# A two-layer transformer kernel: set-up buffers in another order, denser value blocks, other orders in its first and last iterations

## The reference

```
m = silu(mod) @ w_ada + b_ada                    # 9 vectors per batch: shifts, scales, gates
h = ln(x)*(1+sc)+sh; x += self_attn(h)*g         # windows of 128 rows, shifted by 64      (stage A)
h = ln(x)*(1+sc)+sh; x += topk_cross_attn(h)*g   # 77 context rows, softmax over the 16 largest scores (stage B)
h = ln(x)*(1+sc)+sh; x += swiglu(h)*g            # 256 -> 2*1024 -> 256                     (stage C)
xq = ada_ln(x); xkv = ada_ln(context)
x = x + cross_attn(xq, xkv) @ Wp + bp            # plain softmax over 77 context rows       (stage D)
```

## Time and profile before

| | us |
|---|---|
| runs, median of 3 | 1008.47 |
| profiled execution, own time | 1009.15 |
| its span, first to last instruction | 1007.0 |
| PE busy in the span | 955.5 |
| DVE busy | 851.8 |
| ACT busy | 782.0 |
| POOL busy | 682.3 |

### The profile page before, as it was taken

One profiled execution on the slowest core, in us unless ns is written; L12 is line 12 of the kernel. 1 busy time (PEld: TensorE's weight loads), 2 busy tenths in 40 slices (PEclk: granted clock), 3 DMA queues, 4 the chain that ended last, 5 costly groups with the idle time before them and its releaser, 6 DMA issues.

```text
span 1007.0 us, 32855 instructions
## 1 busy us (share of the span) xinstructions
PE 955.5 (95%) x10750; PEld 836.9 (83%) x10750; DVE 851.8 (85%) x4268; ACT 782.0 (78%) x1679; POOL 682.3 (68%) x1092
## 2 busy tenths in 40 slices
PE   6776899999999999999999999999999999999996
PEld 3564688899988888989898888888999888887784
DVE  1467899999999999999999999999999999889643
ACT  1244678888888888888888888888888888887764
POOL 1158356877777777777777777777777777777763
PEclk9678999999999999999999999999999999999999
DMA  8255400000000000000100011000100100000000
GB/s 281 67 97 89 143 22 7 14 21 23 23 24 23 23 24 13 17 18 23 24 23 23 23 23 23 18 11 19 23 23 23 23 23 18 18 7 7 7 7 16
DMA packets 72153, 33.66 MB, mean 33 GB/s; under 512 B 56520, under 2 KB 68961, under 8 KB 71346
## 3 DMA queue, kind: packets, MB, share of 16 engines
q1 hardware_dynamic: 71986, 31.57, 12.6%
HBM read 22.64 MB, written 8.91 MB: 31 GB/s over the span
## 4 chain that ended last, share of the span: by engine, by line
PE 84%; issue 5%; DVE 4%; POOL 4%; ACT 2%; DMA 0%; DVEq 0%; SPq 0%; POOLq 0%; ACTq 0%
PE ps L2211 22%; PE ps L2222 10%; PE ps L2090 8%; PE ps L2200 8%; PE ps L2176 7%; PE ps L2189 6%; PE ps L2162 4%; PE ps L2138 3%; PE ps L2121 3%; PE ps L2151 3%; PE ps L2101 3%; PE ps L2111 2%; PE ps L2079 2%; PE ps L2011 1%; DVE mx_A L1412 1%
## 5 line engine op out<-in xcount | busy, mean ns | idle before, releaser
L2211 PE MATMUL ps<-hT_C,w_m_sb 128*128 128x128 f32 x2048 | 264.5, 278 | 1.2 <-DVE hidden_C L1555 0.8
L2211 PEld LDWEIGHTS ps<-hT_C,w_m_sb 128*128 128x128 f32 x2048 | 247.4, 192 | 13.7 <-issue 6.8
L934 ACT ACTIVATE silu_C<-ps,cols_sb 128x128 f32<-128x128 f32 x256 | 93.5, 367 | 71.8 <-PE ps L2211 67.7
L2222 PE MATMUL ps<-w_m_sb,hidden_C 128*128 128x256 f32 x512 | 121.1, 379 | 0.0
L601 POOL TENSOR_TENSOR p_B<-p_B,rc_B 128x616 f32<-128x616 f32 x64 | 77.8, 1217 | 51.3 <-DVE p_B L1473 50.7
L1465 DVE MATCH_REPLACE8 scores_left_B<-mx_B,scores_left_B 128x77 f32<-128x77 f32 x512 | 107.7, 223 | 0.0
L1461 DVE MATCH_REPLACE8 scores_left_B<-mx_B,scores_B 128x77 f32<-128x77 f32 x512 | 107.3, 224 | 0.0
L2222 PEld LDWEIGHTS ps<-w_m_sb,hidden_C 128*128 128x128 f32 x512 | 92.4, 190 | 9.9
L1412 DVE TENSOR_REDUCE mx_A<-ps 128x8 f32<-128x1024 f32 x64 | 75.5, 1221 | 22.6 <-PE ps L2121 22.6
L1555 DVE SCALAR_TENSOR_TENSOR hidden_C<-ps,cols_sb,silu_C 128x128 f32<-128x128 f32 x256 | 83.3, 337 | 10.1 <-ACT silu_C L934 9.8
L601 POOL TENSOR_TENSOR p_D<-scores_D,rc_D 128x616 f32<-128x616 f32 x63 | 76.8, 1222 | 16.2 <-DVE rc_D L1510 9.3
(11 more groups left out here) (187 smaller groups left out, 2520.6 us busy)
## 6 DMA issues: line engine op xcount, KB each, us to landing
xn_turned<-xn_blocks_A SPq DMA_DIRECT2D x124, 32.0 KB, 2.0
xn_A<-xn_turned SPq DMA_DIRECT2D x31, 128.0 KB, 2.1
x_A<-in_x SPq DMA_DIRECT2D x28, 128.0 KB, 2.4
out<-y_D SPq DMA_DIRECT2D x28, 128.0 KB, 2.4
w_m_sb<-in_w_m SPq DMA_DIRECT2D x3, 1024.0 KB, 7.9
w_mod_sb<-in_w_mod SPq DMA_DIRECT2D x2, 1024.0 KB, 11.0
gate_b<-row_tables SPq DMA_DIRECT2D x3, 512.0 KB, 5.2
gate<-row_tables SPq DMA_DIRECT2D x2, 512.0 KB, 4.2
```

The lines of the kernel that those rows point to most:

```text
L934: sc.activation(SA[:, j, :], bank(f"C.up{j}")[:, 0:P], ACT.Silu, bias=col("bm1_a", j)).then_inc(sa_ok, 1)
L2211: ins = mm(bank(f"C.up{j}")[:, half * P:(half + 1) * P], w_m1[:, k, m:m + P], HT["C"][:, t % HT_COPIES["C"], k, :], start=(k == 0), stop=( ...
L2222: ins = mm(bank("C.dn0")[:, 0:CH], G[:, t % G_COPIES, j, :], w_m2[:, j, :], start=(j == 0), stop=(j == HJ - 1))
```

## The change

It has four parts.

1. The order of the set-up buffers in the second `early` group. `rows` and `w_kv["B"]` move; `w_kv["B"]` (and with it the weights of D, loaded over it) no longer lies under PT["B"] and x_C but under the pads of D; R, PT["B"], x_C, xn_C lie over buffers that the bias set-up reads last.
2. Each first writer waits for what lies below it: `weights_t(0, "B")` for `gb_done` and `tables_out`, `modulate(0, "C")` and `add_bias(0, "C")` for the keys and values of B, `hidden(0, 0)` and `add_residual(0)` for `wo_done`; only D's first writers wait for `pad_ok`, given by a new POOL step `clear_pads()`, much later.
3. `vblk[s]` is [P, 4, 512] for [P, BATCH, NCH, 2, QUAD], 2048 for 2560 columns, without blocks for pairs that a chunk does not touch. POOL fills it by ten instructions (a chunk row and a half of the heads each, all batches) for four; the masks are made by five copies for ten, in a step of their own at the start.
4. `fill()` and `drain()` of all five engines in new orders; `body(i)` is unchanged on each.

```diff
-        vblk = {s: sb(f"vblk_{s}", [P, BATCH, NCH, 2, QUAD]) for s in "BD"}
+        vblk = {s: sb(f"vblk_{s}", [P, 4, 512]) for s in "BD"}
...
             def set_up_values(s):
+                pool.wait_ge(vmask_ok, HCH)
                 pool.wait_ge(v_in[s], 16 * (KC + 1) * BATCH)
-                for b in range(BATCH):
-                    ins = g.tensor_tensor(vblk[s][:, b].rearrange("p c m (n d) -> p c (m n) d", n=2),
-                                          vf[s][:, b].unsqueeze(2).to_broadcast([P, NCH, 4, HD]),
-                                          pair_mask[:].unsqueeze(3).to_broadcast([P, NCH, 4, HD]), ALU.mult)
+                for m in range(HCH):
+                    w = CHUNK_WIDTH[m]
+                    for c in range(KC):
+                        src = vf[s][:, :, c * HCH + m, :]
+                        where = vblk[s][:, VALUE_BANK[m], VALUE_COL[m]:VALUE_COL[m] + KC * BATCH * w]
+                        ins = g.tensor_tensor(where.rearrange("p (b c j d) -> p c b j d", b=BATCH, c=KC, d=HD)[:, c],
...
+            def clear_pads():
+                pool.wait_ge(kb_done["D"], 1)
+                pool.wait_ge(vb_done["D"], 1)
+                pool.wait_ge(v_out["D"], 16 * BATCH)
+                pool.wait_ge(wo_done, 2)
+                pool.wait_ge(kbias_ok, KBIAS)
```

More of the change, by code:

```diff
@@ L47 @@
 PT_HALVES = [0, 1, 1]
+CHUNK_WIDTH = [2 * HD * len(CHUNK_PAIRS[m]) for m in range(HCH)]
+VALUE_BANK = [3, 0, 1, 2, 3]
+VALUE_COL = [0, 0, 0, 0, KC * BATCH * CHUNK_WIDTH[0]]
 SCALE = 1.0 / float(HD) ** 0.5
@@ L720, in drain @@
                 fold_sums(TILES - 7)
-                add_bias(TILES - 7, "D")
-                normalise_weights(TILES - 7, "D", 0)
-                add_bias(TILES - 6, "D")
-                less_max(TILES - 3, "B", 0)
-                divide_a(TILES - 2)
-                add_bias(TILES - 4, "B")
-                add_bias(TILES - 5, "C")
+                normalise_weights(TILES - 7, "D", 0)
+                add_bias(TILES - 4, "B")
+                less_max(TILES - 3, "B", 0)
+                normalise_weights(TILES - 7, "D", 1)
@@ L728, in drain @@
+                divide_a(TILES - 2)
+                reciprocal_root(TILES - 4, "C")
+                add_bias(TILES - 5, "C")
+                less_max(TILES - 6, "D", 0)
+                add_bias(TILES - 7, "D")
+                less_max(TILES - 3, "B", 1)
                 add_bias(TILES - 4, "C")
-                normalise_weights(TILES - 7, "D", 1)
-                reciprocal_root(TILES - 4, "C")
-                less_max(TILES - 6, "D", 0)
                 top_less_max(TILES - 3)
-                less_max(TILES - 3, "B", 1)
@@ L843, in modulate @@
                     act.wait_ge(mod_done, LN[s] + 1)
+                if first(t) and s == "C":
+                    act.wait_ge(kb_done["B"], 1)
+                    act.wait_ge(v_out["B"], 16 * BATCH)
+                    act.wait_ge(vb_done["B"], 1)
                 for c in range(KC):
@@ L982, in fill @@
                 exponentials(1, "B", 0)
+                top_exponentials(1)
+                key_blocks(3)
+                values(3)
+                queries(3, "A")
+                normalise(2, "B")
+                exponentials(1, "B", 1)
+                modulate(2, "B")
                 normalise(4, "A")
-                key_blocks(3)
-                top_exponentials(1)
+                queries(2, "B")
                 normalise(0, "C")
-                queries(3, "A")
-                values(3)
@@ L1001, in fill @@
                 output_t(1, "B")
+                exponentials(2, "B", 0)
                 silu(0, 0)
@@ L1552, in hidden @@
                 dve.wait_ge(sa_ok, HJ * t + j + 1)
+                if first(t) and j == 0:
+                    dve.wait_ge(wo_done, 2)
+                    dve.wait_ge(ct_ps, 1)
+                    dve.wait_ge(vb_done["B"], 1)
                 if t >= G_COPIES:
@@ L1616, in fill @@
                 statistics(1, "B")
+                turn_input(3)
+                row_sums(0, "B")
+                set_up_output_weights(1)
                 keep_chosen(0, 1)
@@ L1731, in fill @@
                 maxima_a(5, 1)
+                turn_input(6)
                 add_maxima(5)
-                statistics(7, "A")
-                turn_input(6)
+                select(4, 1, 0)
+                select(4, 3, 0)
                 select(4, 0, 0)
                 select(4, 2, 0)
-                select(4, 3, 0)
-                select(4, 1, 0)
             def body(i):
@@ L2325, in fill @@
                 up(1, 4)
+                project_o(4, "A")
                 up(1, 5)
```

890 lines of the change are left out of this document (446 added, 444 removed).

## The result

The changed kernel takes 1000.06 us (median of 7 runs, 996.91 to 1003.74), the kernel before 1009.28 beside it (7 runs, 1004.64 to 1009.93): ratio 0.9922, 95% interval 0.9903 to 0.9942. Forecast 998.5, range 991 to 1006. The profiled execution of after is its fastest: 996.91 us, span 994.8, 3.2 us under the median; what follows from its trace is the change in its best execution.

A forecast was written before the change was run, and what follows sets the result against it. PE bounds the kernel, full from 200 us; DVE paces 60 to 117 us. 1009.15 - 12.5 (first iterations) + 0.5 (`w_m2`) + 3.0 (unplaced) - 1.0 (last iterations) = 999.2, less 0.7 for the median: 998.5 us, range 991 to 1006.

The forecast's parts named there:

- Step 1: First iterations up to tile 1's scores: tile 1's input turned earlier so projections fill PE's waits; -4.5 us.
- The tables about 6 us later cost nothing: `write_tables` behind `move_input(1)`: tables about 6 us later, but first user `set_up_output_weights(0)` stands behind modulation at 42.
- Step 2: Tile 0's selection on DVE: B's value blocks moved later on POOL, idle removed, 27.8 us becomes 23.8; -4.0 us.
- The blocks at 4.4 us: POOL's making of `vblk_B`: 4.0 us for 2048 columns, six more instructions at 0.05 to 0.1 each; 4.4 us.
- Step 3: Tile 1's selection on DVE up to `up(0,0)`: 23.9 us becomes 20.2; -3.7 us.
- the wait for `w_m1`: At `up(0,0)`: second half of `w_m1` issued at 99, landing at 107, so start at 107 instead of 106.
- Step 4: `w_m2` queued behind `move_input(4)` lands late for `down(0,0)`: cost 0 to 4.6 us, taken as +0.5.
- R3: Rival, SP's queue: `add_maxima(3)` stays put, `w_m1` and `w_m2` land late; slower, 1014 us; chance 0.07.
- The allowance: First iterations: engine hand-overs and PE at 1.2 GHz that couldn't be placed, bounds 0 and 8; +3.0 us.
- R1: Rival, the clock comes back: closer work in the first iterations also removes low-clock time; 992 us; chance 0.15.
- Step 5: Last iterations: PE's gaps can be filled, the `maxima_in_psum` swap stays hidden; bounds -3.4 and +0.8, taken as -1.0 us.
- R2: Rival: DVE's new order waits as long in other places, little gain left; 1005.5 us; chance 0.15.

The follow-up runs named there:

- e1: Changed kernel with the last iterations (`drain()` of all five engines) in the order of the kernel before; 993.5 us, ratio 0.9861 to the kernel before.
- e2: Kernel before with only the last iterations (`drain()` of all five engines) in the new order; 1015.7 us, ratio 1.0088 to the kernel before.
- e12: Changed kernel with tile 1's early input turn, projections and modulation steps put back later on DVE, ACT and PE; 1013.4 us, ratio 1.0068 to the kernel before.
- e4: Changed kernel with `project_q(0,A)` back ahead of the gate product on PE; 999.4 us, ratio 0.9932 to the kernel before.
- e9: Changed kernel with value blocks as before: four instructions, 2560 columns, instead of ten, 2048; 998.3 us, ratio 0.9906 to the kernel before.
- e6: Changed kernel with `scores_t(31)` ahead of the second `transpose_p(29,B)` in PE's last iterations; 1000.6 us, ratio 0.9932 to the kernel before.
- e7: Changed kernel with only DVE's list of the last iterations as in the kernel before; 996.5 us, ratio 0.9910 to the kernel before.
- e11: Changed kernel with the old last iterations, except both `maxima_in_psum(31)` ahead of `less_max_from_psum(31,0)` on DVE; 989.0 us, ratio 0.9836 to the kernel before.
- e5: Changed kernel with both `normalise_weights(30,B)` ahead of `reciprocal_root(28,D)` in POOL's last iterations; 1001.3 us, ratio 0.9944 to the kernel before.
- e3: Changed kernel with POOL's `set_up_values` of B back between `less_max(0,B,0)` and `add_bias(0,B)`; 1006.6 us, ratio 0.9993 to the kernel before.
- e8: Changed kernel with `turn_input(1)` on DVE back behind `add_maxima(0)`; 1012.4 us, ratio 1.0050 to the kernel before.
- e10: Changed kernel with `weights_t(0,B)` waiting for `pad_ok`, and D's keys, values and pads made early on POOL; 1022.0 us, ratio 1.0135 to the kernel before.

## Why the prediction came out right, step by step

The time was right, and the mechanism of the larger part too, but two errors cancel, which is luck: the first iterations gave more than forecast, through the clock, and the last took where they should have given.

**Step 1 (-4.5) was right in its order and left out the clock.** `scores_a(1)` moved by 10.3 us (e1) to 11.7. But the profile of before overstates the move: e2, with the same first iterations, has it at 53.1 and `up(0,0)` at 116.2, 3.2 us earlier. Most of that is the gate product, whose weights arrive at another moment in each execution: it ends at 18.4 us before and at 16.3 in e2, and in the kernels with the new first iterations between 15.8 and 18.2. So e1 is better set beside e2. The gates end 0.5 us earlier. From there to `scores_t(0)` it is 17.0 and 16.8 us. The projections and modulation 2 ahead of `weigh_values_a(0)` cost 1.2 net of the wait that they fill. From there to `scores_a(1)` it is 7.9 less: 4.5 for `project_k`, `project_q`, `project_v` and modulation 2, 1.1 for the wait behind B's values, and 2.5 for `weigh_values_a(0)` and `set_up_values("B")` at a higher clock (1.08 and 3.68 us for 1.93 and 5.36), less 0.2 of small steps. By order that is 4.0 us; another 2.5 are clock, which this step held at nothing.

Those 2.5 us come with the filled wait. In the three executions in which PE waits 2.7 or 2.8 us ahead of `weigh_values_a(0)` (before, e2, e12) the clock falls to 0.50 in the wait and the two steps take 1.93 to 1.94 and 5.31 to 5.46 us. In the eleven without it the first takes 1.08 in ten and the second 3.68 in eight.

`project_q(0,"A")` ahead of the gates or behind makes no difference (e4), as forecast. "The tables about 6 us later cost nothing" was argued with the wrong first user (e12); it held only because the turn came early.

**Step 2 (-4.0) was right in kind.** Tile 0's selection to tile 1's takes 25.0 us, not 27.8: -2.8. DVE's idle fell from 6.5 to 0.9 as said, but 2.9 us of work came into the stretch, not 1.5. The blocks at 4.4 us was wrong: 4.90, without effect (e9). No row had the 0.05 to 0.1 us put for each further instruction; the six cost 0.15 each beside the 4.0 us that the columns give.

**Step 3 (-3.7) was right:** 19.1 to 19.9 us, not 23.9. Its end was wrong. The three steps add to -12.2 and to 107.3 for `up(0,0)`, not 106, so the wait for `w_m1` that brought it to 107 added nothing even on paper. It didn't come: the second half was issued at 92.19, not 99, because `add_bias(3,A)` had shifted with step 1's larger gain. At `up(0,0)` it is -16.0 (e1) to -20.4 us against the profile of before, and -12.8 to -17.2 against e2, where -12.5 was forecast.

**Step 4 (+0.5):** transfer 4.94 us, `w_m2` issued at 105.19, `down(0,0)` at 113.48 without a wait. 0. R3 is out.

**The allowance (+3.0) had the wrong sign, and R1 is half right.** Hand-overs and low clock were to cost 3 us; nothing of it shows at `up(0,0)`, and low-clock time went. The profiled executions with after's first iterations (e4 and e9 have one edit in them) fall in two kinds. Where the clock of 18 to 56 us was 0.91 or 1.00 (after, e6, e7, e11), `up(0,0)` stands at 98.5 to 99.2; where it was 0.78 to 0.87 (e1, e4, e5, e9), at 103.5 to 104.3. So the clock there is worth 5 us. The times of all executions say the same of the whole: of the 54 of these eight kernels 15 had a mean clock of 0.995 or more, of the 61 of the kernel before beside e1 to e12 none had over 0.986. Within e6, five executions at 0.995 to 0.998 took 996.0 to 997.4 us and five at 0.985 took 1002.5 to 1006.1. The change thus lets the full clock come back, but in some executions only, and the median of after is of the other kind. R1's price was also wrong by its own words: half of the 13.9 us is 7, not 3.5, which gives 988.5.

The Trainium skill, page "TensorE: Matmul & The Clock Gate", section "HAM oscillation — how this bites in real kernels", has the clock fall with waits between bursts. The wait of 2.7 us above agrees; the 2.2 us of idle ahead of the gates did not bring it down in the profiled execution (1.00 from 12 to 26 us), and the same first lists get 0.82 (e5) or 1.00 (e11) between 18 and 56 us, so the rule alone doesn't tell which. What decides it stays open.

**Step 5 (-1.0, bounds -3.4 and +0.8) failed.** It is +8 us: 1.7 ahead of `scores_a(31)` and about 6 in D1 (e1, e2). "The gaps of PE can be filled" was taken for "will be". The new order has more gaps, of 0.8 to 2.2 us behind POOL, ACT and DVE. The 1.7 us are DVE's order (e7). Of the 6, none of three edits gave back more than 0.3, so that loss is not one of these waits; what in the mutual order of the lists makes it stays open.

The sum by measured terms, at e1's clock: -16.0 up to `up(0,0)`, -0.5 from there to `scores_a(31)` with the old drain, +1.7 and +6 in the new one: -8.8, against -9.2 by the medians of after's group. R2 is out: DVE waits less in its new order, not as long in other places.

## What to carry to other kernels

In lists of steps that nothing reorders, price a move by what stands behind it on every engine: one wait in a place where its input is late cost 6 to 22 us here (e3, e8, e10), and the same step placed when its input is there cost nothing. Judge the parts of a change apart: 16 us won at the start hid 8 us lost at the end, and the same start with the old end (e1, e11) is 7 to 11 us faster than after. A gap seen in PE's timeline is worth its length only if the engine behind it has slack. Measure a stretch between two fixed steps rather than the whole time: D1 agrees within 1.4 us over ten kernels, where whole times of one differ by 7 to 10. But choose the stretch so that it holds all that was changed: D1 starts behind the first 1.7 us of the loss. And before a trace is called "before", look at a second one of the same lists: two of the old first iterations stand 3.2 us apart at `up(0,0)`.

## What the chip showed that I had not expected

The same first iterations, run in six kernels (after, e1, e5, e6, e7, e11), reach `up(0,0)` up to 5.8 us apart (98.5 to 104.3), with granted clocks of 0.82 to 1.00 between 18 and 56 us. Ten POOL multiplications over 128 or 256 columns, 2048 in all, take as long as four over 640 (4.90 and 4.96 us).
